# A decoder layer with attention and experts: sums with the queries one slot sooner on VectorE

## The chip, the cores and the metric

The kernel runs on one core of a Trainium2 chip. The metric is the device time of one execution in microseconds (us); the median of several runs is compared.

## The reference, cut to what matters

The input x is 32 sequences of 256 tokens with 256 channels, in float32. The layer has three parts, each followed by a layer norm:

```python
x = layernorm(x + recurrence(x))            # state = x + state * decay over the sequences, times x
Qp, Kp, Vp = relu(x @ Wq + bq), relu(ctx @ Wk + bk), relu(ctx @ Wv + bv)
out = softmax(q @ k.T / 4) @ v              # 16 heads of 16 channels
x = layernorm(x + ln_g * norm(out + Qp) + ln_b)
xn = rms_norm(x) * scale
ids = argmin(|xn|^2 + |centroid|^2 - 2 xn @ centroid.T)     # one of 8 experts for each token
x = layernorm(x + expert[ids](xn))          # up, silu gate, down
```

The recurrence runs over the first axis, so that sequence n needs the state that sequence n-1 left. The change touches the second part (`out + Qp` and its norm) and the choice of the expert (`ids`).

## The kernel before, in words

There are two phases. Phase 1 does the recurrence, the attention and the choice of the expert for all 32 sequences, and writes each token's row into the bucket of its expert in HBM. Phase 2 runs the experts over 71 tiles of 128 rows. The change is in phase 1 alone.

Phase 1 is a software pipeline over sequences, unrolled. In step t, the engines work on several sequences at once: the scores of sequence t (`cur`), the probabilities of t-1 (`prv`), the division, the sum with the queries and the norm of t-2 (`a`), and the choice of the expert of t-3 (`b`); the recurrence and projections are ahead (`nn` is t+2). Each step has 16 slots h, one for each head. On every engine the order of instructions is written out by hand: a function `step(t)` with a loop over h and `if h == ...` lines. Engines meet through semaphores alone. An instruction waits on its engine until the counter is reached, and what stands behind it on that engine waits too.

What VectorE does in a step (the code is printed below):

- `maxima(cur, h)` takes the maximum over the keys for head h from the score bank `S_ps[h % 2]` in PSUM (L1559). It comes in pairs, for h and h+1 at each even h. So all that stands in slots 4 and 5 is issued behind maxima 4 and 5, what stands in 6 and 7 behind maxima 6 and 7, and so on. TensorE's scores of head h+2 overwrite the bank and wait for maximum h.
- h == 3: `u` is (state + 1) times the input (L1577), an operation of two tiles in SBUF.
- h == 4 and 5: statistics and moments of u (L1543, L1549), `divide(a, 0, ...)`: a reciprocal of the sums of the probabilities (L1747) and the product with it (L1750), for the first 128 tokens; `divide(a, 1, ...)` is for the other 128, at h == 7.
- `add_queries(a, c)` (L1758) adds the queries, `oq = o + qn`, 128 x 256 elements, both tiles in SBUF. It waits for the division of the same half.
- `pick(b, 0)` to `pick(b, 5)`: the distances to the 8 centroids (L1776, two instructions), the least of them (L1780), the candidates (L1783, L1787), the choice (L1790) and the one-hot matrix (L1793). All are small, and each waits for the one before it.
- h == 9: statistics and moments of oq (`stx`, `mvx`). GpSimd makes the inverse deviation `rsx` from them.
- h == 11 and 12: `slots(b, 0)` to `slots(b, 3)`, the last of which (L1813) gives the place of each token in its bucket, after TensorE's `ranks(b)`, which needs the one-hot; `gain` and `add_first` for sequence a.
- h == 13 and 14: x1 of sequence nn, statistics of y2.

GpSimd's order in a step is: `by_re`, the products of the recurrence (L782); `xw` (L840); the bias into x1 (L879); `q_lo`, the low part of the queries (L871); the offsets of the distances (L862); a part of the state (L790); `rs` (L815, L817); the state times its decay (L798); `k_lo` (L871); the state again (L801); `rsx` (L815, L817); two indirect DMAs that scatter the rows into the buckets (L852), which wait for the slots of VectorE; the input into the state (L808); `rs` and `ms` of the next rows (L815 to L832). Most read and write 128 x 512 elements in SBUF.

TensorE does scores and transposed scores of two heads at each even h, and between them flips, projections and the weighted sums. At h == 9 it flips the maxima of the first eight heads, at h == 10 it does `ranks(b)`.

Of the kernel before, what the change touches and what calls it, by code (L numbers as in the profile page):

```python
# [84 lines left out]
def build(nc, x, ctx_in, lmlg, theta, last_conv, Wq, bq, Wk, bk, Wv, bv, ln_g, ln_b, ffn_scale, centroids, up_w, down_w, out):  # L85
    stack = ExitStack()
    with stack:
# [74 lines left out]
        oq = sb1("oq", [P, NTC, C])  # L162
# [32 lines left out]
        stx = sb1("stx", [P, NTC, 6])  # L195
# [41 lines left out]
        def wait(eng, name, item, per=1, j=None):  # L237

            if not item.runtime and item.k >= SEQ:
                item, j = Item(0, SEQ - 1), per  # L240
            wait_value(eng, name, item.times(per, per if j is None else j))
# [28 lines left out]
        def active(item):  # L270
            return item.within(0, SEQ)
# [343 lines left out]
        with nc.Block() as block:  # L615
# [845 lines left out]
            def _(dve):  # L1461
# [100 lines left out]
                def step(t):  # L1562
                    cur, prv, nn, a, b = t, t - 1, t + 2, t - 2, t - 3
                    if t.k == -2:
                        first_state()
                    for h in range(H):
                        if h % 2 == 0:
                            maxima(cur, h)
                            maxima(cur, h + 1)
                        if h == 0 and active(b):  # L1570
                            write_rows(b)
                        if h == 3 and active(nn):

                            wait(dve, "x1_ok", nn - 1, 2)
                            wait(dve, "conv", nn, 5)
                            wait_ring(dve, x_in[nn.mod(2)], nn, 2, 16)
                            v.scalar_tensor_tensor(u[:, :, :], state[:, 0], 1.0, xt[:, nn.mod(2)], ALU.add, ALU.mult).then_inc(s["u_ok"], 1)  # L1577
                        if h == 4 and active(nn):
                            wait(dve, "u_ok", nn)
                            wait(dve, "rstd1", nn - 1, 2)  # L1580
                            stats(nn, u, st1, "ln1")
                        if h == 5:
                            if active(a):
                                divide(a, 0, 0)
                            if active(nn):
                                moments(nn, st1, mv1, "ln1")
                            if active(a):
                                divide(a, 0, 1)
                        if h == 6 and active(b):
                            pick(b, 0)  # L1590
                        if h == 7:
                            if active(a):
                                divide(a, 1, 0)
                            if active(b):
                                pick(b, 1)
                            if active(a):
                                divide(a, 1, 1)
                            if active(b):
                                pick(b, 2)
                            if active(a):  # L1600
                                add_queries(a, 0)
                            if active(b):
                                pick(b, 3)
                        if h == 8:
                            if active(b):
                                pick(b, 4)
                            if active(a):
                                add_queries(a, 1)
                            if active(b):
                                pick(b, 5)  # L1610
                        if h == 9 and active(a):
                            wait(dve, "oq_ok", a, 2)
                            stats(a, oq, stx, "lnx")
                            moments(a, stx, mvx, "lnx")
                        if h == 11:
                            if active(b):
                                slots(b, 0)
                            if active(a):
                                gain(a, 0)
                            if active(b):  # L1620
                                slots(b, 1)
                            if active(a):
                                gain(a, 1)
                            if active(b):
                                slots(b, 2)
                        if h == 12:
                            if active(b):
                                slots(b, 3)
                            if active(a):
                                add_first(a)  # L1630
                        if h == 13 and active(nn):
                            wait(dve, "rstd1", nn, 2)
                            wait(dve, "y_ok", nn - 4, 4)
                            for c in range(NTC):
                                v.tensor_scalar(x1[:, nn.mod(4), c], u[:, c], mv1[:, c, 0:1], rs1[:, 1, c:c + 1],  # L1635
                                                ALU.subtract, ALU.mult).then_inc(s["x1_ok"], 1)
                        if h == 14 and t.k == -2:
                            bias_pieces()
                        if h == 15 and t.k == -2:
                            first_key_cut()  # L1640
                        if h == 1 and t.k == -1:
                            first_cuts()
                        if h == 5 and t.k == 0:
                            centroids_scaled()
                        if h == 11 and t.k == 0:
                            centroids_squared()
                        if h == 13 and active(a):
                            wait(dve, "y_ok", a, 4)
                            stats(a, y2, st2, "ln2")
                        if h == 14 and active(a):  # L1650
                            moments(a, st2, mv2, "ln2")
                        for e in LO_AT.get((t.k, h), ()):
                            lower(e)
# [99 lines left out]
                def add_queries(a, c):  # L1753

                    if c == 0:
                        wait(dve, "qn_ok", a)
                    wait(dve, "o_ok", a, 4, 2 * c + 2)
                    v.tensor_tensor(oq[:, c].rearrange("p (o h w) -> p o h w", o=NCH, h=HPC),  # L1758
                                    o[:, c].rearrange("p (o h w) -> p o h w", o=NCH, h=HPC),
                                    qn[:, a.mod(4), c].rearrange("p (o w h) -> p o h w", o=NCH, h=HPC),  # L1760
                                    ALU.add).then_inc(s["oq_ok"], 1)
# [6 lines left out]
                def pick(b, stage):  # L1768

                    ch = choice[:, :].unsqueeze(2).to_broadcast([P, NTC, E])  # L1770
                    if stage == 0:
                        wait(dve, "dist_pe", b)
                        wait(dve, "rms", b, 4)
                        wait(dve, "offset", b)
                        for c in range(NTC):
                            v.scalar_tensor_tensor(dist[:, 1, c], M_ps[2][:, c * E:(c + 1) * E], row[:, b.mod(2), c, C:C + 1], dist[:, 0, c],  # L1776
                                                   ALU.mult, ALU.add).then_inc(s["pick"], 1)
                    if stage == 1:
                        wait(dve, "pick", b, PICK, 2)
                        v.tensor_reduce(least[:, :], dist[:, 1], AX.X, ALU.min).then_inc(s["pick"], 1)  # L1780
                    if stage == 2:
                        wait(dve, "pick", b, PICK, 3)
                        v.tensor_tensor(cand[:, 0], dist[:, 1], least[:, :].unsqueeze(2).to_broadcast([P, NTC, E]), ALU.is_gt)\  # L1783
                            .then_inc(s["pick"], 1)
                    if stage == 3:
                        wait(dve, "pick", b, PICK, 4)
                        v.scalar_tensor_tensor(cand[:, 1], cand[:, 0], float(E), expert_no[:, :, :], ALU.mult, ALU.add).then_inc(s["pick"], 1)  # L1787
                    if stage == 4:
                        wait(dve, "pick", b, PICK, 5)
                        v.tensor_reduce(choice[:, :], cand[:, 1], AX.X, ALU.min).then_inc(s["slot_ok"], 1)  # L1790
                    if stage == 5:
                        wait(dve, "slot_ok", b, SLOT, 1)
                        v.tensor_tensor(onehot_bf[:, :, :], expert_no[:, :, :], ch, ALU.is_equal).then_inc(s["pick"], 1)  # L1793
# [56 lines left out]
```

## Time and profile before

| | us |
|---|---|
| median of 3 runs (1195.03 to 1201.86) | 1198.85 |
| profiled execution | 1206.74 |
| its span, first to last instruction | 1205.0 |
| TensorE busy, matmuls | 1114.3 |
| VectorE busy | 955.2 |
| GpSimd busy | 770.5 |
| ScalarE busy | 668.3 |

The profile is of one execution. Busy time is the union of the engine's instructions. An instruction that waits for a semaphore hasn't begun and counts as idle; one that has begun and is held up inside shows as a longer duration. Phase 1 takes about the first 790 us; the 27 sequences from 105.2 to 738.6 us take 633.4 / 27 = 23.5 us each.

### The profile page before, as it was taken

To read this page: it belongs to the slowest core of one execution; us is meant where nothing else is said; L and a number is where in the kernel's file an instruction comes from. 1 tells how busy PE (TensorE), PEld (TensorE's weight loads), DVE (VectorE), ACT (ScalarE), POOL (GpSimd) and SP (SyncE) were. 2 spreads that over 40 slices of the span, in tenths; PEclk is the share of its full clock that TensorE was granted. 3 is DMA by queue.
4 is the path that set the end of the run, shared out by engine and by line. 5 is a ranking of instruction groups with operands and counts; after the bars stand their busy time and mean duration, and the time that the engine had idled before them with its cause. 6 is when DMAs were issued, how large, how long until landed. Compare 5 with 4: busy or idle time off the path is not lost.

```text
span 1205.0 us, 27881 instructions
## 1 busy us (share of the span) xinstructions
PE 1114.3 (92%) x8283; PEld 831.0 (69%) x8315; DVE 955.2 (79%) x2437; ACT 668.3 (55%) x1417; POOL 770.5 (64%) x933
## 2 busy tenths in 40 slices
PE   4899999989989999999999999989999999999996
PEld 3776666666666666666666666668788888888885
DVE  7569999999998898899999999888755555555553
ACT  4277677677766676777777677663222222222221
POOL 4748798879978887889889884245433333333333
PEclk9999999999999999999999999889999999999998
DMA  4776676666677567766656555203554445444442
GB/s 127 184 168 155 168 156 162 164 169 151 157 162 170 150 146 164 168 161 176 163 157 170 148 130 126 51 17 119 175 158 149 147 145 155 152 153 150 147 150 89
DMA packets 126529, 178.05 MB, mean 148 GB/s; under 512 B 14054, under 2 KB 111983, under 8 KB 120208
## 3 DMA queue, kind: packets, MB, share of 16 engines
q1 hardware_dynamic: 119888, 159.65, 52.0%
q0 software_dynamic: 6528, 16.99, 4.6%
q8 instruction: 59, 0.97, 0.4%
q14 instruction: 54, 0.44, 0.1%
HBM read 124.47 MB, written 53.03 MB: 147 GB/s over the span
## 4 chain that ended last, share of the span: by engine, by line
PE 43%; DVE 30%; issue 9%; DMA 7%; POOL 6%; SPq 3%; ACT 1%; POOLq 0%; DVEq 0%; ACTq 0%
DVE neg_max_sb L1559 12%; PE Y L489 10%; PE G L451 8%; PE A L451 8%; DVE oq L1758 3%; DVE u L1577 3%; PE S L1232 3%; DMA neg_max<-nm_row 3%; PE M L1189 3%; PE GT L461 2%; PE O L1181 2%; DMA q_pieces<-q_lo 2%; POOL buckets L852 2%; POOL state L808 2%; DVE stx L1543 1%
## 5 line engine op out<-in xcount | busy, mean ns | idle before, releaser
L1559 DVE TENSOR_REDUCE neg_max_sb<-S 128x2 f32<-128x512 f32 x512 | 328.4, 683 | 46.2 <-PE S L1232 44.6
L1022 ACT ACTIVATE probs<-T 128x512 f32<-128x512 f32 x512 | 278.0, 595 | 144.9 <-PE T L1245 125.8
L1232 PE MATMUL S<-k_st,q_st 48*128 48x256 f32 x1024 | 209.7, 313 | 31.7 <-DVE neg_max_sb L1559 28.8
L1245 PE MATMUL T<-q_st,k_st 49*128 49x256 f32 x1024 | 206.5, 314 | 8.6 <-DMA q_st<-neg_max 5.5
L1232 PEld LDWEIGHTS S<-k_st,q_st 48*128 48x128 f32 x1024 | 142.3, 187 | 102.2 <-issue 71.9
L1245 PEld LDWEIGHTS T<-q_st,k_st 49*128 49x128 f32 x1024 | 142.8, 188 | 23.9 <-ACT probs L1022 13.2
L429 ACT ACTIVATE gT<-GT 128x512 f32<-128x512 f32 x71 | 42.5, 598 | 205.6 <-PE GT L461 202.3
L1181 PE MATMUL O<-probs,v_aug 128*32 128x256 f32 x2048 | 142.7, 398 | 0.7 <-ACT probs L1022 0.7
L409 POOL DMA_INDIRECT out<-res,token x71 | 76.0, 1070 | 102.1 <-DVE res L576 97.0
L489 PE MATMUL Y<-dn_sb,gT 128*128 128x256 f32 x568 | 134.6, 380 | 1.4 <-ACT gT L429 0.7
L852 POOL DMA_INDIRECT buckets<-row,slot x64 | 67.1, 1048 | 87.3 <-DVE slot L1813 76.3
L489 PEld LDWEIGHTS Y<-dn_sb,gT 128*128 128x128 f32 x568 | 107.1, 189 | 20.4 <-DMA dn_sb<-in_L_ffn_down_w 2.3
L451 PE MATMUL G<-up_hi,xsT 128*128 x284 | 106.7, 416 | 0.4 <-issue 0.4
L451 PE MATMUL A<-up_hi,xsT 128*128 x284 | 106.4, 415 | 0.0
L576 DVE TENSOR_SCALAR res<-y,mv,rs 128x256 f32<-128x256 f32 x71 | 29.4, 413 | 78.3 <-POOL rs L416 78.2
L414 POOL TENSOR_SCALAR rs<-mv 128x1 f32<-128x1 f32 x71 | 16.6, 234 | 116.1 <-DVE mv L605 115.1
L1181 PEld LDWEIGHTS O<-probs,v_aug 128*32 128x32 f32 x2048 | 54.8, 112 | 51.4 <-ACT probs L1022 15.5
L1189 PE MATMUL M<-ctT,wk_sb 128*128 128x256 f32 x256 | 65.0, 398 | 13.9 <-issue 7.6
L433 ACT ACTIVATE gate<-G 128x512 f32<-128x512 f32 x71 | 42.4, 597 | 57.6 <-PE G L451 57.6
L782 POOL TENSOR_TENSOR by_re<-state,decay 128x1024 f32<-128x1024 f32 x31 | 73.5, 2372 | 1.1 <-DVE x L1635 0.9
L1208 PE MATMUL M<-wv_sb,ctT 128*128 128x256 f32 x256 | 68.4, 391 | 4.4 <-ACT k L1121 1.9
L1189 PE MATMUL M<-x1T,wq_sb 128*128 128x256 f32 x256 | 65.9, 401 | 1.3 <-ACT x1T L1089 1.3
(212 smaller groups left out, 2579.8 us busy)
## 6 DMA issues: line engine op xcount, KB each, us to landing
dn_sb<-in_L_ffn_down_w SPq DMA_DIRECT2D x71, 512.0 KB
k_st<-k_pieces SPq DMA_DIRECT2D x64, 256.0 KB
q_st<-q_pieces SPq DMA_DIRECT2D x64, 256.0 KB
xr<-buckets SPq DMA_DIRECT2D x71, 129.0 KB
xt<-in_x SPq DMA_DIRECT2D x32, 256.0 KB, 6.7
ct<-in_ctx SPq DMA_DIRECT2D x32, 256.0 KB, 7.1
k_pieces<-k_hi SPq DMA_DIRECT2D x32, 256.0 KB
k_pieces<-k_lo SPq DMA_DIRECT2D x32, 256.0 KB
```

What stands on the lines that cost most here:

```text
L409: g.indirect_dma_start(out=out_rows, out_offset=bass.IndirectOffsetOnAxis(ap=token[:, f.mod(2):f.mod(2) + 1], axis=0), in_=res[:, f.mod(2) ...
L451: last = t_.matmul(ps[:, :], xT[:, w, c * P:(c + 1) * P], src[:, bass.ds(off + c * 2 * HID, HID)], start=(k == 0), stop=(k == len(terms) - 1))
L489: last = t_.matmul(Y_ps[:, 0:C], gT[:, m.mod(2), c * P:(c + 1) * P], dn_sb[:, m.mod(2), c * C:(c + 1) * C], start=(c == 0), stop=(c == HCH ...
L782: g.tensor_tensor(by_re[:, :, :, :], state[:, 0].unsqueeze(1).to_broadcast(both), pair_b, ALU.mult).then_inc(s["conv"], 1)
L852: g.indirect_dma_start(out=buckets[:, :], out_offset=bass.IndirectOffsetOnAxis(ap=slot[:, p, c:c + 1], axis=0), in_=row[:, p, c, :], in_of ...
L1022: a_.activation(probs[:, h % 8].rearrange("p k t -> p (k t)"), T_ps[h % 2][:, :], ACT.Exp, scale=DH ** -0.5).then_inc(s["exp_ok"], 1)
L1181: last = t_.matmul(O_ps[32 * j:32 * j + 32, (grp % 2) * TOK:(grp % 2 + 1) * TOK], v_aug[:, item.mod(4), kc, h * VW:h * VW + 32], probs[:, ...
L1189: last = t_.matmul(dst[:, oc * TOK:(oc + 1) * TOK], w[:, ic, oc * P:(oc + 1) * P], xT[:, ic, :], start=(ic == 0), stop=(ic == NCH - 1))
L1208: last = t_.matmul(M_ps[1][:, c * C:(c + 1) * C], ctT[:, ic, c * P:(c + 1) * P], wv_sb[:, ic, :], start=False, stop=(c == NTC - 1 and ic = ...
L1232: last = t_.matmul(S_ps[h % 2][:, c * TOK:(c + 1) * TOK], q_st[h // HPC][base:base + STACK, h % HPC, c * P:(c + 1) * P], k_st[h // HPC][ba ...
L1245: last = t_.matmul(T_ps[h % 2][:, c * TOK:(c + 1) * TOK], k_st[h // HPC][base:base + AUG, h % HPC, c * P:(c + 1) * P], q_st[h // HPC][base ...
L1559: v.tensor_reduce(neg_max[:, cur.mod(2), :, h], S_ps[h % 2][:, :].rearrange("p (c t) -> p c t", c=NTC), AX.X, ALU.max, negate=True).then_i ...
```

## The change

The diff moves calls within VectorE's `step`; the functions called stay as they are, and no other engine's code changes.

```diff
                             if active(a):
                                 divide(a, 0, 1)
-                        if h == 6 and active(b):
-                            pick(b, 0)
+                                add_queries(a, 0)
                         if h == 7:
                             if active(a):
                                 divide(a, 1, 0)
                             if active(b):
-                                pick(b, 1)
+                                pick(b, 0)
                             if active(a):
                                 divide(a, 1, 1)
                             if active(b):
+                                pick(b, 1)
                                 pick(b, 2)
                             if active(a):
-                                add_queries(a, 0)
+                                add_queries(a, 1)
                             if active(b):
                                 pick(b, 3)
-                        if h == 8:
+                        if h == 9:
                             if active(b):
                                 pick(b, 4)
                             if active(a):
-                                add_queries(a, 1)
+                                wait(dve, "oq_ok", a, 2)
+                                stats(a, oq, stx, "lnx")
                             if active(b):
                                 pick(b, 5)
-                        if h == 9 and active(a):
-                            wait(dve, "oq_ok", a, 2)
-                            stats(a, oq, stx, "lnx")
-                            moments(a, stx, mvx, "lnx")
+                            if active(a):
+                                moments(a, stx, mvx, "lnx")
```

Before, the order behind maxima 6 and 7 is: distances (two), reciprocal, least, product, cand, first sum, cand; behind maxima 8 and 9: choice, second sum, one-hot, two statistics, two aggregates. After, the first sum is behind the product of the first half, ahead of maximum 6. Behind maxima 6 and 7 stand: reciprocal, distances, product, least, cand, second sum, cand; behind 8 and 9: choice, two statistics, one-hot, two aggregates. The product u stays where it is, at h == 3, behind maxima 2 and 3 and ahead of maximum 4.

## Rows read from the trace of the kernel before

**Rows 1.** Chain of waits, 646 to 670 us: start, us, what.
```profile
650.48 2.01 DVE u L1577
...
665.75 0.08 DVE slot L1813
...
669.00 1.30 POOL state L808
```
**Rows 2.** Busy time by stretch; the header is the first row.
```profile
core 0: us, PE busy (x) PEld busy (x) DVE busy (x) ACT busy (x) POOL busy (x), PEclk, DMA share, GB/s
105.20:738.60 633.40, 585.50 (x5216) 404.13 (x5244) 593.61 (x1514) 453.24 (x999) 536.35 (x590) 0.99 0.66 159
413.00:415.50 2.50, 2.50 (x20) 0.89 (x20) 0.87 (x3) 0.85 (x2) 2.17 (x6) 0.50 0.76 185
```
**Rows 3.** Waits of TensorE, 105.2 to 738.6: total us, times, longest.
```profile
PE S L1232 <- DVE neg_max_sb L1559: 26.9, 33, 1.1
```
**Rows 4.** Groups of VectorE, 105.2 to 738.6: busy us, mean ns | idle before.
```profile
L1758 DVE TENSOR_TENSOR oq<-o,qn 128x256 f32<-128x256 f32 x54 | 51.5, 954 | 0.0
...
L1793 DVE TENSOR_TENSOR onehot_bf<-expert_no,choice 128x16 bf16<-128x16 f32 x27 | 15.6, 577 | 0.0
```
**Rows 5.** Timeline of VectorE, 652.8 to 662.8: start, duration.
```profile
655.09 0.39 DVE L1750 TENSOR_TENSOR o<-M,rden 128x256 f32<-128x256 f32 x1
655.40 1.28 DVE L1559 TENSOR_REDUCE neg_max_sb<-S 128x2 f32<-128x512 f32 x2
...
657.62 0.23 DVE L1783 TENSOR_TENSOR cand<-dist,least 128x16 f32<-128x16 f32 x1
657.77 0.66 DVE L1758 TENSOR_TENSOR oq<-o,qn 128x256 f32<-128x256 f32 x1
658.35 0.17 DVE L1787 SCALAR_TENSOR_TENSOR cand<-cand,expert_no 128x16 f32<-128x16 f32 x1
658.43 1.28 DVE L1559 TENSOR_REDUCE neg_max_sb<-S 128x2 f32<-128x512 f32 x2
659.63 0.16 DVE L1790 TENSOR_REDUCE choice<-cand 128x2 f32<-128x16 f32 x1
659.70 1.37 DVE L1758 TENSOR_TENSOR oq<-o,qn 128x256 f32<-128x256 f32 x1
660.96 0.20 DVE L1793 TENSOR_TENSOR onehot_bf<-expert_no,choice 128x16 bf16<-128x16 f32 x1
661.11 0.76 DVE L1543 BATCH_NORM_STATS2 stx<-oq 128x6 f32<-128x256 f32 x2
662.02 0.25 DVE L1549 BATCH_NORM_AGGREGATE mvx<-stx 128x2 f32<-128x6 f32 x2 [0.16 <-DVE stx L1543]
662.18 1.26 DVE L1559 TENSOR_REDUCE neg_max_sb<-S 128x2 f32<-128x512 f32 x2
```
**Rows 6.** Timeline of GpSimd, 649.5 to 664.9.
```profile
649.99 2.37 POOL L782 TENSOR_TENSOR by_re<-state,decay 128x1024 f32<-128x1024 f32 x1
...
655.14 1.27 POOL L871 TENSOR_TENSOR q_lo<-q,q_hi 128x512 fp32r<-128x512 f32 x1
...
657.78 0.73 POOL L815 TENSOR_SCALAR rs<-mv 128x2 f32<-128x2 f32 x1
...
659.27 1.28 POOL L798 TENSOR_TENSOR state<-state,decay 128x512 f32<-128x512 f32 x1
660.52 1.78 POOL L871 TENSOR_TENSOR k_lo<-k,k_hi 128x512 fp32r<-128x512 f32 x1
```
**Rows 7.** Timeline of VectorE in a slower sequence, 612.5 to 616.9.
```profile
612.66 1.42 DVE L1758 TENSOR_TENSOR oq<-o,qn 128x256 f32<-128x256 f32 x1
613.98 1.27 DVE L1793 TENSOR_TENSOR onehot_bf<-expert_no,choice 128x16 bf16<-128x16 f32 x1
```
**Rows 8.** Timeline of GpSimd in the same sequence, 611.5 to 617.
```profile
613.54 1.68 POOL L871 TENSOR_TENSOR k_lo<-k,k_hi 128x512 fp32r<-128x512 f32 x1
```
**Rows 9.** Timeline of VectorE in another sequence, 420 to 422.
```profile
421.16 0.39 DVE L1750 TENSOR_TENSOR o<-M,rden 128x256 f32<-128x256 f32 x1
```
**Rows 10.** Timeline of GpSimd in that sequence, 420 to 422.
```profile
420.23 1.27 POOL L871 TENSOR_TENSOR q_lo<-q,q_hi 128x512 fp32r<-128x512 f32 x1
```

## The prediction, written before the changed kernel had run

> **What bounds the kernel now.** I read the chain of waits first, for one sequence in the middle of the attention phase. It runs almost wholly on VectorE: from the state product u, through the maxima, to the cast of the slots at 665.75. There it crosses to GpSimd, which starts the two scatters and then adds the input into the state at 669.00, and so comes round to the next sequence [rows 1]. Everything VectorE does ahead of the slots is therefore on the path, one instruction behind the other; what it does behind them is not. The stretch of 27 sequences confirms it: VectorE is busy 593.61 of 633.40 us, TensorE 585.50 [rows 2], and TensorE's commonest wait in it is for VectorE's maxima, 26.9 us [rows 3].
>
> Then I read the groups of VectorE in that stretch. Two of them have means that are too long for their size. The sum with the queries takes 954 ns on average but 0.66 us in one place of the sample sequence and 1.37 us in another; the one-hot takes 577 ns on average for 16 elements, 0.20 us in the sample and 1.27 us in another sequence [rows 4, 5, 7]. Beside GpSimd's timeline the reason is plain. The second sum starts at 659.70 and ends at 661.07, 0.52 us behind the end of GpSimd's state product (659.27 + 1.28 = 660.55). GpSimd's k_lo in turn takes 1.78 us where q_lo, of the same size, takes 1.27 [rows 5, 6]. In the slow sequence k_lo (613.54 + 1.68 = 615.22) and the one-hot (613.98 + 1.27 = 615.25) end together [rows 7, 8]. So the sums, the one-hot and the small comparisons of two tiles in SBUF take turns with GpSimd's operations, each whole; the statistics, maxima and divisions (of PSUM or one tile) show no such wait.
>
> **The change part by part.** No instruction is added or removed. Per sequence the first sum goes from behind maximum 7 to behind maximum 5; the second from behind maximum 9 to behind maximum 7; the statistics of the sum go ahead of the one-hot; the first distances go behind the reciprocal. No DMA moves and no queue of SP or GpSimd is reordered. Since all of it is ahead of the slots, only three things count: how long the moved instructions take at their new places, gaps between dependent instructions, and what GpSimd does meanwhile. I work it out on the sample sequence, whose maxima 6 to 10 start at 655.40, 658.43 and 662.18 (6.78 us from 6 to 10) [rows 5].
>
> *First sum, behind maximum 5.* It is ready when the division ends, 655.09 + 0.39 = 655.48 [rows 5]. GpSimd's q_lo has the turn from 655.14 to 656.41 [rows 6]. By the 0.52 us above the sum ends at 656.93, and maximum 6 starts at 656.85 (VectorE's next instruction starts some 0.08 before the last one's end) instead of 655.40: 1.45 us later. Bounds: 0.6 if it need not wait (0.66 us in its old place), 1.8 if it waits for the whole of q_lo (1.27 + 0.52). I take 1.45; 22 of the 27 sequences have the division's end inside q_lo as here. In the other five, as at 421.16 + 0.39 = 421.55, q_lo (420.23 + 1.27 = 421.50) is just over [rows 9, 10], and the sum costs its 0.6.
>
> *GpSimd.* The sum holds it up by some 0.45 us (k_lo's 1.78 against 1.27), but the sum that left block 7 no longer holds up its rs (0.73 us at 657.78). So its state product L798, at 659.27 before, starts at 659.2: unmoved [rows 6].
>
> *Block 7 (behind maximum 7).* The second sum is where the first was, so the 3.03 us from maximum 6 to 8 stay if it gets its turn, and maximum 8 starts at 656.85 + 3.03 = 659.88. But VectorE now comes here 1.45 us later against a GpSimd that has not moved. The comparison cand, at 657.62 before, comes at 659.07, or up to 0.16 later, since the least distance and cand now stand directly behind each other (0.16 us is what such a pair costs at the statistics and their aggregate [rows 5]). The sum follows at 659.2 to 659.3, just as L798 wants the turn, and then the second cand, with L798 waiting. Who loses waits: L798 until 660.5, plus 0.52, puts the sum's end at 661.0 instead of 659.85, 1.15 us; if only the second cand loses, L798 runs 659.8 to 661.05, again about 1.15. Bounds: 0, and 2.4 where both turns are lost. How often? The old one-hot stands in just this position, directly behind a sum with k_lo waiting. Its mean of 577 ns between the levels 190 and 1270 says that it lost (577 - 190) / (1270 - 190) = 36% of its turns [rows 4, 5, 7]. One such turn is certain here and one may be, so between 0.36 and 1 - 0.64 x 0.64 = 0.59; I take 0.45.
>
> *Block 9.* With the turns won, maximum 8 at 659.88, the choice 1.20 later, 0.07 for it, 0.68 for both statistics: the one-hot is ready at 661.83. GpSimd runs L798 from 659.9 to 661.15 and k_lo to 662.42. So the one-hot waits again and ends at 662.45; the aggregate no longer shows its own 0.16 gap; maximum 10 starts at 662.53. The second sum's 1.37 is gone from here, but the one-hot takes 0.62.
>
> *Sum.* From the old maximum 6 to the new maximum 10, 7.13 us with the turns won. The old mean is the sample's 6.78, plus 0.38 for the one-hot (577 against 200), less 0.12 for the sums (2 x 954 against 660 + 1370): 7.04 [rows 4, 5]. That is +0.09 x 27 = +2.4 us; the five sequences without the wait at the first sum give back about 0.5 each, -2.5. So with all turns won the change is worth nothing: 0. The lost turns add 27 x 0.45 x 1.15 = 14 us. The profiled execution takes 1206.74 us, with 1.74 outside its span, 8 above the median; 1206.74 + 14 = 1221, and on the median 1198.85 + 14 = 1213 us.
>
> TensorE waits with VectorE: S8 needs maximum 6 (at 657.53), S10 needs maximum 8. It has that time, since it waited for maxima before and the end of the sequence is set by the slots. The drain and the first sequences, where GpSimd is not in step, I leave at nothing.
>
> The Trainium skill (SBUF — State Buffer, Who interferes with whom) has a rule for these turns: a VectorE instruction with two SBUF inputs and a GpSimd instruction that reads SBUF exclude each other, the one that issues first keeps the port for its whole length, and the other blocks fully. The waits above agree. Taken to the letter it says more: an operation that already waits asked first and should always go next, and that is the second rival. The one-hot's mean of 577 ns [rows 4] speaks against the letter, since it would then be 1.27 us in every sequence.
>
> **The rivals.**
> *All turns won, no change* (1199 us, -4 to +4). For it: the first cand and the old first sum stood back to back while GpSimd's rs waited, and at 657.77 the sum went through [rows 5, 6]. Against: the one-hot's 36%.
> *All turns lost.* GpSimd, waiting since 659.2, always goes ahead of the next VectorE instruction: 27 x 1.15 = +31, 1230 us. Against: the one-hot's mean.
> *Faster, the other side.* The first sum does not wait at its new place. It decides at 655.14 against 655.48: were the division done 0.34 us sooner, or q_lo started that much later, the sum would cost 0.6 and not 1.45, maximum 6 to 10 shrink by 0.85 x 22 = 19 us, with a third of the lost turns left: 1198.85 - 19 + 5 = 1185. For it: the second sum, whose waits are the dearest, leaves its place under L798, and five sequences already show the favourable order [rows 9, 10]. Against: 22 of 27, and both engines are set in step by u, which has to wait for GpSimd's by_re (649.99 + 2.37 = 652.36) and ends shortly behind it [rows 1, 6], so the 0.34 us won't drift.
> *TensorE's clock.* Where the sum loses, S10 comes 1.9 us late. At 413.00 to 415.50 the granted clock was 0.50, the lower of the two levels, 1.2 GHz, with TensorE busy throughout; its waits for maxima, up to 1.1 us long, come once or twice in each sequence [rows 2, 3]. Half speed for 2.5 us costs 1.25. One more such drop in each of the 12 losing sequences would make it +14 + 15, 1228 us. It belongs to the upper end.
>
> **How the numbers follow.** Some turns lost, 1206 to 1222 around 1213: 0.45. All lost, or the clock with it, about 1229: 0.17. No change, 1193 to 1205: 0.23. Faster, about 1185: 0.15. A difference of 0.5% (6 us) is about what can be told from none. So slower 0.62, same 0.23, faster 0.15. The range from 1194 to 1232 leaves out most of the faster case and a little above.
>
> **What would show it.** The first sum at about 1.45 us, ending 0.5 behind q_lo, in some 22 of 27 sequences; the second sum in two groups, 0.65 and about 1.8 us (or the second cand at 0.16 and 1.27); the one-hot near 0.6 and seldom 0.2; the idle time ahead of the aggregate gone; the chain still crossing to GpSimd at the slots. If the first sum takes 0.65 throughout, the forecast is wrong, and the kernel faster. If the turns in block 7 are always won, it stays where it was.

## The result and the profile after

The changed kernel takes 1233.7 us in the median of 4 runs (1229.23 to 1233.94), before 1200.36 us (4 runs). The ratio is 1.0259, 95% interval 1.0222 to 1.0296: slower, 33 us. The forecast was slower, 1213 us, with a range from 1194 to 1232: the direction came true, but 14 of the 33 us were forecast, and the time lies just above the range. The ratios, here and below, leave out executions more than 1.5% above the fastest of their kernel, while the medians hold all of them. The runs of the kernel before that the experiments are compared with have medians of 1200.95 to 1203.83 us.

The profiled execution took 1229.23 us with a span of 1227.5, and the one before 1206.74 us. That is 22.5 us between them and not 33: the profile after is of the fastest of its four executions, and the one before lies 8 us above the 1198.85 us of its table. The traces can therefore show where the time goes, but not all of the 33 us.

The chain of waits of one sequence, 546 to 570 us, answers to [rows 1]. It still crosses from VectorE's slots to GpSimd, and the second cand (cand L1786) now stands in it with 1.17 us, where it took 0.09 before (the numbers of the lines behind the change are one lower):

```profile
550.06 2.01 DVE u L1577
...
558.47 0.17 DVE cand L1782
...
559.20 1.17 DVE cand L1786
...
566.46 0.08 DVE slot L1812
...
569.74 1.29 POOL state L808
```

The groups of VectorE from 106.3 to 741 us (26 sequences) answer to [rows 4]. The sums cost together what they did (972 against 954 ns); the second cand has gone from 166 to 1169 ns. The last number, the idle time before it, is 0.0, so no list of waits shows this:

```profile
L1757 DVE TENSOR_TENSOR oq<-o,qn 128x256 f32<-128x256 f32 x52 | 50.5, 972 | 2.7
L1786 DVE SCALAR_TENSOR_TENSOR cand<-cand,expert_no 128x16 f32<-128x16 f32 x26 | 30.4, 1169 | 0.0
L1792 DVE TENSOR_TENSOR onehot_bf<-expert_no,choice 128x16 bf16<-128x16 f32 x26 | 16.0, 616 | 0.0
```

VectorE's timeline of one sequence, 555 to 562.9, answers to [rows 5]:

```profile
554.67 0.39 DVE L1749 TENSOR_TENSOR o<-M,rden 128x256 f32<-128x256 f32 x1
555.17 1.32 DVE L1757 TENSOR_TENSOR oq<-o,qn 128x256 f32<-128x256 f32 x1
556.41 1.27 DVE L1559 TENSOR_REDUCE neg_max_sb<-S 128x2 f32<-128x512 f32 x2
...
558.47 0.17 DVE L1782 TENSOR_TENSOR cand<-dist,least 128x16 f32<-128x16 f32 x1
558.57 0.63 DVE L1757 TENSOR_TENSOR oq<-o,qn 128x256 f32<-128x256 f32 x1
559.12 1.25 DVE L1786 SCALAR_TENSOR_TENSOR cand<-cand,expert_no 128x16 f32<-128x16 f32 x1
560.29 1.28 DVE L1559 TENSOR_REDUCE neg_max_sb<-S 128x2 f32<-128x512 f32 x2
...
562.22 0.61 DVE L1792 TENSOR_TENSOR onehot_bf<-expert_no,choice 128x16 bf16<-128x16 f32 x1
562.75 0.23 DVE L1549 BATCH_NORM_AGGREGATE mvx<-stx 128x2 f32<-128x6 f32 x2
```

And GpSimd's beside it, which answers to [rows 6]:

```profile
554.73 1.27 POOL L871 TENSOR_TENSOR q_lo<-q,q_hi 128x512 fp32r<-128x512 f32 x1
555.97 0.61 POOL L862 TENSOR_TENSOR dist<-cent_norm,nx 128x16 f32<-128x16 f32 x1
...
558.74 1.59 POOL L798 TENSOR_TENSOR state<-state,decay 128x512 f32<-128x512 f32 x1
560.30 1.26 POOL L871 TENSOR_TENSOR k_lo<-k,k_hi 128x512 fp32r<-128x512 f32 x1
```

Read them together. q_lo holds the first sum up until 556.00; the sum ends 0.49 us later. The second sum gets its turn and takes 0.63 us, L798 waits for it from 558.74, and takes 1.59 instead of 1.27 us. Then L798 goes ahead of cand, which ends at 560.37, 0.04 behind L798. In all 26 sequences the first sum takes 1.20 to 1.33 us, and in 24 of them cand is as long as here.

The two others matter, since their times of asking are the same. In this one L798 asked 0.38 us ahead of cand, as above, and cand went first all the same (VectorE, then GpSimd):

```profile
168.04 0.17 DVE L1786 SCALAR_TENSOR_TENSOR cand<-cand,expert_no 128x16 f32<-128x16 f32 x1
```
```profile
167.66 1.70 POOL L798 TENSOR_TENSOR state<-state,decay 128x512 f32<-128x512 f32 x1
```

The second thing is TensorE. Its waits for maxima in 106.3 to 741 (answering to [rows 3]) are 48.5 us, where they were 26.9:

```profile
PE S L1232 <- DVE neg_max_sb L1559: 48.5, 50, 1.5
```

And its granted clock is lower: the busy time by stretch, the columns as in [rows 2], 0.97 against 0.99 in the mean, and 0.50 in one drop.

```profile
106.30:741.00 634.70, 570.41 (x5048) 391.35 (x5046) 600.80 (x1459) 439.55 (x962) 509.92 (x572) 0.97 0.64 154
```
```profile
611.40:614.80 3.40, 3.40 (x19) 2.25 (x15) 2.42 (x9) 0.90 (x2) 0.78 (x2) 0.50 0.36 104
```

There are eleven such drops of 3.4 us between 106 and 741 us, three in the kernel before (the thirteen that an expectation below speaks of hold two more, behind 741). During this one the timeline of TensorE has four matmuls for the values at 1.91 us, where they take 1.02 at full clock, and VectorE waits 0.98 us for the scores of head 12:

```profile
611.75 1.91 PE L1208 MATMUL M<-wv_sb,ctT 128*128 128x256 f32 x4
```
```profile
614.42 1.29 DVE L1559 TENSOR_REDUCE neg_max_sb<-S 128x2 f32<-128x512 f32 x2 [0.98 <-PE S L1232]
```

Most sequences take 24.08 us now; eight take 25.1 to 25.4, each with a drop in it. The mean is 24.41, before it was 23.46. Eight of the eleven drops begin 0.6 to 2.3 us behind the end of a wait of 1.46 us for maximum 8; the other three (164.2, 188.1, 311.0) do not, there the nearest wait is one of 0.4 us.

### The profile page after: what moved, and what is told of

Same layout as the page of the kernel before. It is cut to its first block, busy times and chain, and to the rows that moved or that the text cites. A ratio compares the mean times of both kernels' runs of the same rounds, so it can differ in the third digit from the quotient of the medians.

```text
span 1227.5 us, 27912 instructions
## 1 busy us (share of the span) xinstructions
PE 1117.5 (91%) x8314; PEld 830.7 (68%) x8315; DVE 984.2 (80%) x2437; ACT 672.1 (55%) x1417; POOL 756.2 (62%) x933
## 4 chain that ended last, share of the span: by engine, by line
PE 44%; DVE 35%; issue 9%; POOL 7%; DMA 2%; SPq 2%; ACT 1%; POOLq 0%; DVEq 0%; ACTq 0%
DVE neg_max_sb L1559 13%; PE Y L489 10%; PE G L451 8%; PE A L451 8%; DVE oq L1757 4%; DVE u L1577 4%; PE S L1232 3%; PE O L1181 3%; POOL buckets L852 2%; POOL state L808 2%; PE GT L461 2%; PE M L1189 2%; DVE cand L1786 2%; DVE st L1543 2%; PE M L1208 2%
## 5 line engine op out<-in xcount | busy, mean ns | idle before, releaser
L1232 PE MATMUL S<-k_st,q_st 48*128 48x256 f32 x1024 | 212.8, 314 | 57.1 <-DVE neg_max_sb L1559 51.7
L1245 PE MATMUL T<-q_st,k_st 49*128 49x256 f32 x1024 | 209.8, 316 | 2.0 <-ACT probs L1022 1.8
L1189 PE MATMUL M<-ctT,wk_sb 128*128 128x256 f32 x256 | 69.7, 420 | 17.3 <-issue 9.9
L1208 PE MATMUL M<-wv_sb,ctT 128*128 128x256 f32 x256 | 73.7, 414 | 0.0
L1189 PEld LDWEIGHTS M<-ctT,wk_sb 128*128 128x128 f32 x256 | 50.1, 206 | 29.5 <-issue 14.6
```

What stands on the lines that cost most here:

```text
L1189: last = t_.matmul(dst[:, oc * TOK:(oc + 1) * TOK], w[:, ic, oc * P:(oc + 1) * P], xT[:, ic, :], start=(ic == 0), stop=(ic == NCH - 1))
L1208: last = t_.matmul(M_ps[1][:, c * C:(c + 1) * C], ctT[:, ic, c * P:(c + 1) * P], wv_sb[:, ic, :], start=False, stop=(c == NTC - 1 and ic = ...
L1232: last = t_.matmul(S_ps[h % 2][:, c * TOK:(c + 1) * TOK], q_st[h // HPC][base:base + STACK, h % HPC, c * P:(c + 1) * P], k_st[h // HPC][ba ...
L1245: last = t_.matmul(T_ps[h % 2][:, c * TOK:(c + 1) * TOK], k_st[h // HPC][base:base + AUG, h % HPC, c * P:(c + 1) * P], q_st[h // HPC][base ...
```

## The experiments

Theory A is the forecast's own: VectorE's operations with two SBUF tiles take turns with GpSimd's, and the loss is a lost turn of the second cand. Theory B is its rival: the loss is the first sum's wait behind q_lo.

**The first sum alone** moved (an edit of the kernel before; the second sum stays behind maximum 9, the distances in their old order):

```diff
                                 divide(a, 0, 1)
+                                add_queries(a, 0)
...
-                                add_queries(a, 0)
                             if active(b):
                                 pick(b, 3)
```

> Only the first sum moves, to behind maximum 5; the second stays behind maximum 9 ahead of the one-hot, the distances stay in their old order. Theory A (turns: an operation of VectorE that stands directly behind a sum loses its turn to a waiting GpSimd operation of 128 x 512, 1.1 us each time): the second cand now stands behind the first cand and not behind a sum, so it is short (0.17 us); the first sum takes 1.3 us as in the changed kernel; the one-hot still stands behind the second sum and waits for 1.2 us in a share of the sequences. Maximum 6 is 1.4 us late, block 7 is 0.5 us shorter, so about +0.9 us in each of 27 sequences: 1220 to 1230 us. Theory B (the price of the change is the wait of the first sum behind q_lo alone, 1.2 to 1.4 us a sequence): the same as the changed kernel or more, 1230 to 1240 us, and cand short.

Measured: 1246.92 us, ratio 1.0338 (1.0297 to 1.0379), more than either theory said; taken on the 1198.85 us of the prediction, the ratio gives 1239 us, within B's. The groups of VectorE, 106.3 to 741: cand has its 175 ns, but the sums take 1472 ns in the mean and the one-hot is long nearly always:

```profile
L1757 DVE TENSOR_TENSOR oq<-o,qn 128x256 f32<-128x256 f32 x50 | 73.6, 1472 | 2.6
L1792 DVE TENSOR_TENSOR onehot_bf<-expert_no,choice 128x16 bf16<-128x16 f32 x25 | 29.1, 1162 | 0.0
```

So the lost turns moved to the next candidates. The second sum comes 0.09 us behind k_lo and waits for the whole of it: 572.60 + 1.70 = 574.30 against k_lo's 572.51 + 1.27 = 573.78 in one sequence, and about so in all but the first. The one-hot behind it, which had lost 36% of its turns before, loses about 90% ((1162 - 190) / (1270 - 190)), this time to L801. My share of lost turns was the weak number, here too. That the time fits B's range says nothing for B, since the one-hot and the second sum carry a good part of it.

**The second sum alone** moved (an edit of the changed kernel; the first sum stays behind maximum 7, directly ahead of the second):

```diff
                                 divide(a, 0, 1)
-                                add_queries(a, 0)
...
                             if active(a):
+                                add_queries(a, 0)
                                 add_queries(a, 1)
```

> The changed kernel, but the first sum stays behind maximum 7, directly ahead of the second sum; all else as changed. Theory A: maximum 6 is not late; both sums run at 0.65 us beside GpSimd's small rs and its power; cand is short, since L798 asks some 0.4 us later; the one-hot waits for half of k_lo, 0.6 to 1.0 us. From maximum 6 to 10 about 6.6 us against 7.05 before: 1185 to 1195 us. If cand loses its turn here too: 1205 to 1215. Theory B: maximum 6 is not late, so nothing is lost, and the gain is what the second sum waited behind maximum 9: also faster, 1180 to 1195. It tells whether the second sum's new place alone is good, and so whether the first sum brings the loss.

Measured: 1198.2 us, ratio 0.9953 (0.9919 to 0.9987). Both sums and cand are short:

```profile
L1757 DVE TENSOR_TENSOR oq<-o,qn 128x256 f32<-128x256 f32 x55 | 33.5, 648 | 0.0
...
L1792 DVE TENSOR_TENSOR onehot_bf<-expert_no,choice 128x16 bf16<-128x16 f32 x27 | 18.1, 671 | 0.0
...
L1786 DVE SCALAR_TENSOR_TENSOR cand<-cand,expert_no 128x16 f32<-128x16 f32 x27 | 4.5, 165 | 0.0
```

Two sums of 0.65 us against 1.91 before for both give 0.61 us, the one-hot takes 0.09 back: 0.52 x 27 = 14 us; 6 came. Most sequences take 22.4 or 23.0 us, but six take 23.1 to 27.4, each with a wait of TensorE for the DMA of the negated maxima (0.5 to 2.2 us). The second sum's move does no harm by itself and gains a little; with the first one's the loss comes. It doesn't yet say how.

**The second cand without its turn.** The changed kernel; TensorE copies the expert numbers into PSUM, and cand reads them there, so that one of its operands is in SBUF:

```diff
+                    last = t_.matmul(M_ps[2][:, 128:128 + NTC * E], ident[:, :],
+                                     expert_no[:, :, :].rearrange("p c e -> p (c e)"), start=True, stop=True)
                     last.then_inc(s["dist_pe"], 1)
...
+                    numbers = M_ps[2][:, 128:128 + NTC * E].rearrange("p (c e) -> p c e", c=NTC)
...
-                        v.scalar_tensor_tensor(cand[:, 1], cand[:, 0], float(E), expert_no[:, :, :], ALU.mult, ALU.add).then_inc(s["pick"], 1)
+                        v.scalar_tensor_tensor(cand[:, 1], cand[:, 0], float(E), numbers, ALU.mult, ALU.add).then_inc(s["pick"], 1)
```

> The changed kernel; the expert numbers that the second cand adds are read from PSUM (TensorE copies 16 columns there with one more matmul behind the distances), so that cand has one SBUF operand only and needs no turn. The output is the same. Theory A: cand falls from 1.25 to 0.2 us, maximum 8 comes 1.05 us sooner in 24 of 26 sequences (-25 us), TensorE's wait for S10 falls from 1.6 to 0.5 us, and with it the drops of its clock (13 of 3.4 us in the changed kernel, 3 before), another -5 to -10 us: 1195 to 1205 us, the kernel before. Theory B (the loss is the first sum's wait, and cand's 1.25 us lie beside a wait that VectorE would have anyway): cand falls, the one-hot or a maximum waits instead, 1225 to 1235 us.

Measured: 1194.2 us, ratio 0.9879 (0.9828 to 0.9930), a little better than A's 1195 to 1205. In VectorE's timeline cand takes 0.18 us, and maximum 8 starts 2.78 us behind maximum 6, not 3.88:

```profile
563.10 1.28 DVE L1561 TENSOR_REDUCE neg_max_sb<-S 128x2 f32<-128x512 f32 x2
...
565.25 0.65 DVE L1759 TENSOR_TENSOR oq<-o,qn 128x256 f32<-128x256 f32 x1
565.80 0.18 DVE L1789 SCALAR_TENSOR_TENSOR cand<-cand,M 128x16 f32<-128x16 f32 x1
565.88 1.30 DVE L1561 TENSOR_REDUCE neg_max_sb<-S 128x2 f32<-128x512 f32 x2
```

GpSimd's L798 is there just the same, and waits for the sum:

```profile
565.42 1.62 POOL L798 TENSOR_TENSOR state<-state,decay 128x512 f32<-128x512 f32 x1
```

That settles it between A and B. The first sum still takes 1.31 us in most sequences at its new place, and the kernel is faster than the one before. The loss is cand's lost turn and what follows from it. Most sequences take 22.85 us; four take 26.8 to 27.2, each with a wait of 1.6 to 1.7 us of TensorE for the DMA of the negated maxima and with 6.8 us at half the clock beside it.

**The one-hot ahead of the statistics** in the changed kernel, directly behind the choice:

```diff
+                            if active(b):
+                                pick(b, 5)
                             if active(a):
                                 wait(dve, "oq_ok", a, 2)
                                 stats(a, oq, stx, "lnx")
-                            if active(b):
-                                pick(b, 5)
```

> The changed kernel with the one-hot ahead of the two statistics, directly behind the choice. Theory A: the one-hot asks 0.7 us sooner, at about the moment when k_lo ends and L801 takes over. If L801 is there first, it waits for the whole of it, 1.25 us, and the statistics come behind, maximum 10 some 0.8 us later: 1245 to 1255 us; if it gets in ahead, 0.2 us and 1225 us. Theory C (the statistics ahead of the one-hot are part of the loss, since TensorE's ranks wait for the one-hot): TensorE waits less for the one-hot and the time falls by 5 to 15 us, 1218 to 1229, whatever its duration.

Measured: 1249.11 us, ratio 1.0359 (1.0318 to 1.0400). The one-hot waits for nearly the whole of L801, as A said, and C falls:

```profile
L1792 DVE TENSOR_TENSOR onehot_bf<-expert_no,choice 128x16 bf16<-128x16 f32 x25 | 28.0, 1120 | 0.9
```

So the statistics in front of the one-hot are a good part of the change: behind them it waits for the rest of L801 alone, and takes 0.61 us instead of 1.12.

**Cand and one-hot without turns, in the order before:**

> The order of the kernel before; the expert numbers are copied into PSUM by one more small matmul behind the distances, and the second cand and the one-hot read them there, so neither needs a turn. The output is the same. Theory A (turns): the one-hot falls from a mean of 577 to 190 ns, 0.39 us a sequence on the chain, 10 us over 27 sequences: about 0.99 of before. Theory B (the waits for turns are fillers beside another bound): unchanged, within 0.5%.

Measured: 1199.59 us, ratio 0.9971 (0.9938 to 1.0003), no clear difference, as B said. The profiled execution was the slowest of twelve (1205.27 us, the fastest 1187.07). In it the one-hot fell to 168 ns and most sequences took 22.7 or 22.95 us, but five of 23 took 23.9 to 27.5, four of them with a wait of TensorE of 1.1 to 2.3 us for the DMA of the negated maxima. So the one-hot's saving was there, and those sequences gave it back. A's sum of 10 us came out as 3.5, which isn't clear of zero.

**The same in the changed order:**

> The changed kernel with both the second cand and the one-hot from PSUM (the run with cand alone gave 0.988 of before). Theory A: the one-hot, 0.48 us there, falls to 0.19; most sequences 22.85 - 0.29 = 22.55 us, 8 us in all: 0.98 of before. Against it: the more VectorE gains, the more TensorE waits for the DMA of the negated maxima (four sequences took 26.8 us with cand alone); if those grow, 0.985 to 0.99.

Measured: 1193.91 us, ratio 0.9956 (0.9922 to 0.9991), no better than with cand alone, where 0.98 to 0.99 was expected. Most sequences take 22.72 us, where 22.55 were expected. TensorE waited for that DMA 3 times, with cand alone 9 times, so the waits did not grow. Beside the run before it this is also the comparison of the two orders without the turns of cand and the one-hot: 0.9956 and 0.9971, no difference. What the change costs lies in those turns.

**The sums without turns as well**, beside cand and the one-hot (the division writes over its source in PSUM, TensorE's waits for the banks ask for the sum):

```diff
-                        v.tensor_tensor(o[:, c].rearrange("p (h w) -> p h w", w=DH), src[:, :, 0:DH],
+                        v.tensor_tensor(src[:, :, 0:DH], src[:, :, 0:DH],
...
-                                    o[:, c].rearrange("p (o h w) -> p o h w", o=NCH, h=HPC),
+                                    M_ps[1 - c][:, :].rearrange("p (o h w) -> p o h w", o=NCH, h=HPC)[:, :, :, 0:DH],
```

> As the run before in this call, and the division writes its result over its source in PSUM, from where the sum with the queries reads it; the sums have one SBUF operand and need no turn. TensorE's waits for these banks then ask for the sum instead of the division. Theory A: the first sum falls from 1.3 to about 0.45, the second from 0.65 to 0.45, together 1.05 us a sequence; VectorE would be down to 21.5 us, and TensorE's own work (some 21.4 us a sequence) becomes the bound: 22.0 us a sequence, 0.96 to 0.97 of before. Theory B (the first sum's place costs nothing, since TensorE or a DMA ends last anyway): no more than the run before it.

Measured: 1220.53 us, ratio 1.0152 (1.0117 to 1.0186), a clear miss. The first sum fell as A said, to 0.62 us and not 0.45. TensorE's keys projection, though, now waits for the sum, and the clock of the stretch is 0.96. In the line of the wait, "issue" says that the view names no releaser; the edit does, and the times agree: the first sum ends at 164.84 + 0.62 = 165.46 and the projection starts at 165.56. In the changed kernel the same line is 9.9 us. TensorE's waits and the stretch from 106.3 to 741:

```profile
PE M L1189 <- issue: 20.8, 27, 1.0
```
```profile
106.30:741.00 634.70, 596.20 (x5188) 413.69 (x5188) 560.35 (x1487) 443.37 (x984) 499.20 (x584) 0.96 0.67 157
```

Sequences mostly alternate between 23.0 and 24.7 us, most of the long ones with a drop of the clock (14 in the stretch). VectorE's 40 us less came to nothing. The new wait of TensorE and its clock are what the trace shows in their place; how much of the time each costs was not tested apart.

**The sums alone from PSUM**, cand and one-hot as in the changed kernel:

> The changed kernel with the sums alone from PSUM; the second cand and the one-hot read SBUF as in the changed kernel. It tells whether cand loses its turn because it stands directly behind a sum that holds the turn, or because of when it comes. If behind the sum: the sum holds nothing now, and VectorE comes 0.85 us sooner, so cand comes before L798 asks and is short (0.17 us): 0.97 to 0.985 of before. If cand meets L798 by its own time, it shows 0.5 to 1.25 us: 0.99 to 1.01.

Measured: 1218.01 us, ratio 1.0134 (1.0093 to 1.0175), above both ranges; the keys projection's wait (29.2 us) and 13 drops of the clock are in it too. The sum takes no turn here, and cand waits all the same, 1182 ns in the mean. VectorE:

```profile
522.48 0.60 DVE L1757 TENSOR_TENSOR oq<-M,qn 128x256 f32<-128x256 f32 x1
523.00 1.23 DVE L1786 SCALAR_TENSOR_TENSOR cand<-cand,expert_no 128x16 f32<-128x16 f32 x1
```

and GpSimd:

```profile
522.93 1.27 POOL L798 TENSOR_TENSOR state<-state,decay 128x512 f32<-128x512 f32 x1
```

L798 starts 0.07 us ahead of cand, and 0.06 to 0.11 in nearly every sequence; cand lost in all of them. So the place behind a sum isn't needed to lose the turn: where nobody holds it, the one that comes first takes it. This is not the case of the changed kernel, though, where the sum still holds the turn and both wait for it. Counted from the start of the first sum, cand comes at 3.22 us instead of 3.95, but L798 at 3.15 instead of 3.57, since the sum no longer holds GpSimd up; so L798 is still first.

**The first sum's own price**, both from PSUM, with the first sum behind maximum 7:

> The first sum behind maximum 7 and the second directly behind it (as in the run with the second sum alone moved), with the second cand and the one-hot from PSUM. It differs from the changed kernel with both from PSUM (0.996 of before, 22.72 us in most sequences) only in the place of the first sum. Theory A: the first sum's wait of 0.7 us behind q_lo is gone, most sequences take 22.0 to 22.2 us, 0.975 to 0.985 of before. Theory D (below 22.7 us another bound takes over: TensorE's waits for the DMA of the negated maxima and the drops of its clock that follow): most sequences are shorter but some take 24 to 27 us, and the time is 0.99 to 1.0 of before.

Measured: ratio 0.9919 (0.9876 to 0.9962); the median of all its twelve runs is 1203.26 us. The ratio lies in D's range. The profiled execution was the slowest of the twelve (1210.06 us, the fastest 1184.53), so it shows more of what goes wrong than most. In it the sequences are as D said: two of 23 take 22.25 us, nine take 22.65 to 22.9, and twelve take 23.0 to 27.0. TensorE waits for the DMA that brings the negated maxima 13 times:

```profile
PE T L1245 <- DMA q_st<-neg_max: 13.9, 13, 2.1
```

All these waits lie in the twelve long sequences, and each of the twelve has one. It is the same in the second run (six long sequences, six waits), and in four of the five long ones of the fifth; there the sequences with this wait are those in which VectorE's saving is lost again. It is no floor for a sequence: in the second run seven take 22.4 us without such a wait, and the kernel before has seven such waits too. Why the DMA is late in some sequences and not in others stays open.

**TensorE kept busy** in the changed kernel while it waits for maximum 8:

```diff
+                        if h == 10 and active(b):
+                            for _ in range(4):
+                                t_.matmul(M_ps[2][:, 128:256], ident[:, :], ident[:, :], start=True, stop=True)
                         if h % 2 == 0:
```

> The changed kernel; TensorE does four more matmuls of 128 x 128 ahead of the scores of head 10, into columns of PSUM that nobody reads, about 1.1 us inside its wait of 1.6 us for maximum 8. If the drops of the clock come from that wait: the 13 drops of the changed kernel go down to 5 or fewer, the sequences of 25.1 to 25.4 us become 24.08 like the others, 8 to 12 us in all: 1221 to 1226, 1.016 to 1.02 of before. If the drops have another cause or cost nothing: 1.026 as the changed kernel. The second cand keeps its 1.25 us either way.

Measured: 1224.04 us, ratio 1.0180 (1.0145 to 1.0215), below the changed kernel's interval. Between 106 and 741 there is no drop left:

```profile
106.30:741.00 634.70, 584.83 (x5328) 413.42 (x5328) 609.10 (x1476) 447.40 (x978) 517.09 (x581) 1.00 0.63 156
```

Behind the first, every sequence in the stretch takes 24.0 to 24.1 us, and cand keeps its 1.26. Of the wait of 1.46 us for maximum 8, 0.6 is left. So the drops come with that wait (the three that don't stand directly behind one are gone too), and they cost 1.0259 - 1.0180 = 0.8%, 9.5 us of the 33.

## Why the prediction was wrong

The step that failed is the share of lost turns behind maximum 7, 0.45, which the prediction took from the one-hot's record; measured it is 24 of 26, 0.92. The clock of TensorE behind these lost turns, left out of the sum, is the second part. By its own steps:

- *What bounds the kernel, and the turns.* Right. The long durations of the moved operations end with GpSimd's, the long cand is gone with an operand in PSUM, and the path crosses at the slots.
- *First sum.* Forecast: maximum 6 later by 1.45 us. Measured: 1.43, since it starts 1.35 behind the division's end (556.41 against 555.06) and not 0.08 ahead of it. It waits in all 26 sequences, not in 22 of 27.
- *GpSimd.* Right in the main: L798 asks between the sum's start and the second cand, at 558.74. A sum holds it up by less than the 0.45 us forecast, 0.32 (1.59 against 1.27); k_lo's 1.78 includes the turn of the one-hot that got in ahead of it, and it is 1.68 where the one-hot didn't [rows 6, 8].
- *Block 7.* This step failed. I took the share of lost turns from the one-hot's record, 36% for one turn, 0.45 in all. The second cand lost 24 of 26, 0.92. The engines come in step in every sequence, so that one result repeats, and a share from another place is no chance for this one. The second rival, all turns lost by the rule of the Trainium skill (SBUF — State Buffer, Who interferes with whom), whoever issues first gets the port, came nearest: 1230 us at a chance of 0.17. In this case the trace agrees with it in 24 of 26 sequences, where L798 asks 0.37 to 0.38 us ahead of cand. It does not in the other two, with the same 0.38 us, nor in the kernel before: there k_lo had waited for 0.44 to 0.50 us, and the one-hot got ahead of it in 16 of 25 sequences [rows 5, 6]. So the order of asking doesn't settle the turn where both wait for a sum to end. What does is open, and with it why this place loses so much oftener than the old one.
- *Block 7 and 9, with the turns won.* From the old maximum 6 to the new maximum 10 I had 7.13 us. The run with cand from PSUM has 1.43 + 2.78 + 2.51 = 6.72. Block 7 is 0.25 us shorter than in the old order, as the first cand is no longer held up by L790 and the distances stand closer; so a won turn would have made the kernel faster, by 0.32 x 26 = 8 us, and not the same.
- *The sum.* Measured: 1.43 + 3.88 + 2.62 = 7.93 us against 7.04 (maximum 10 starts 0.16 behind the aggregate at 562.75, so 562.91), 0.89 x 26 = 23 us for the order and the turns. Against the 6.72 us with cand's turn out of the way, a lost turn costs 1.21 us, near the 1.15 of the prediction. That the second rival's 1230 us came so near is in part luck: it had the won case 8 us too high and the clock's 9.5 us not at all.
- *TensorE.* "It has that time" was wrong. The run with the four filling matmuls puts what it lost by its clock behind the wait at 9.5 us. I had this as a rival, priced 1.25 us a drop and one drop in each losing sequence; a drop costs 1.0 to 1.3 us (25.1 to 25.4 against 24.08), but there were eleven in the 26 sequences. It should have been added to the sum of the lost turns, since it follows from them.
- *Both together.* 23 + 9.5 = 32.5 us, near the measured 33. The 23 are counted in one trace and the 9.5 are a difference of ratios, so that they meet so closely is not a proof. What supports the split is the run without drops, 1.0180: 21.6 us are left there, with all the lost turns.

## What to carry to other kernels

Where two engines take turns at a port, work out for each moved operation what the other engine is doing when it asks. If the other's operation is already running, the wait is the rest of it (the first sum in all 26 sequences here). If both wait for a third operation to end, the order of asking didn't settle it here, and a mean over past outcomes at another place is no chance for this one: a schedule that repeats can lose nearly every time. Price a lost turn at the whole length of the other's operation, and add what the engine behind it loses by its clock while it stands. A small operation between two large ones has the most to lose, and giving it an operand in PSUM takes it out of the turns: 0.988 of before here with the first sum, the second sum and the statistics all where the change put them.

## What the runs showed of the hardware

- VectorE's sum of 128 x 256 takes 0.6 to 0.7 us without a wait whether both operands are in SBUF or one is in PSUM (means 0.65 and 0.62); the operand in PSUM only takes away the wait.
- TensorE fell to half its clock for 3.4 us at a time, eleven times in the changed kernel's 26 sequences, in most of which it had waited some 1.5 us for maximum 8. With four small matmuls in that wait, which left 0.6 us of it, it never did. The kernel before, with waits of mostly 0.7 to 1.1 us, had three drops in the same stretch, two of them with a wait for the DMA of the negated maxima close by as well.
- GpSimd is held up by a sum for 0.3 to 0.4 us (1.59 and 1.68 against 1.27), VectorE by GpSimd for up to the whole operation.
- Where both engines wait for VectorE's sum to end and GpSimd has asked first, GpSimd went first in 24 of 26 sequences of the changed kernel and in 9 of 25 of the kernel before, with about the same lead (0.37 to 0.38 and 0.44 to 0.50 us).
